# Attentions: ones beside the values, one set of matmuls for both, the result re-laid through memory

## The chip, the cores and the metric

The kernel runs on 1 core of one Trainium2 chip. The metric is the device time in microseconds (us) of one execution, compared between kernels on the same chip. The engines are called PE (TensorE), DVE (VectorE), ACT (ScalarE), POOL (GpSimd) and SP (SyncE, which only issues DMAs here).

## The reference

A model of four layers on x of 128 batches x 64 tokens x 128 features in f32. Each layer is a gated cross-attention of 16 heads of 8 features, then a gated feed-forward part. The attentions differ in details only (rotary embedding of keys and values in layer 0, biases in layers 1 and 3, a mask in layers 1 and 2); their core is the same:

```
def _L1_xattn_ref(q, k, v, mask, Wq, bq, Wk, bk, Wv, bv, Wo, bo):
    qh = _split_heads(q @ Wq.T + bq)
    kh = _split_heads(k @ Wk.T + bk)
    vh = _split_heads(v @ Wv.T + bv)
    scores = jnp.einsum('bhqd,bhkd->bhqk', qh, kh) * scale
    scores = jnp.where(mask == 0, jnp.float32(-1000000000.0), scores)
    probs = jax.nn.softmax(scores, axis=-1)
    attn = jnp.einsum('bhqk,bhkd->bhqd', probs, vh)
    concat = attn.transpose(0, 2, 1, 3).reshape(q.shape[0], q.shape[1], E)
    return concat @ Wo.T + bo
...
x = x + jnp.tanh(g_xattn[1]) * _L1_xattn_ref(_layernorm(x), ctx, ctx, mask, ...)
x = x + jnp.tanh(g_ffn[1]) * _L1_ffn_ref(_layernorm(x), ...)
```

The feed-forward parts are a routed mixture of experts with a shared expert (layer 0), a dense one (layer 1), a quantised linear one (layer 2) and a routed mixture (layer 3).

## The kernel before, in words

Tokens go in tiles of 128 (two batches), 64 tiles in all, and in chunks of 4 tiles (512 tokens), 16 in all. x stays in SBUF. An attention goes through the chunks in turns; a turn u has four steps s = 0..3, one for each tile, and each engine runs its own list of the turn, with semaphores between them. In layers 1 and 2 most turns stand in hardware loops of two turns (Fori); layers 0 and 3 are written out.

PE's turn (function attention, attention_quantised or attention_routed): at each s the scores of the tile two ahead (psS, L1199), at s = 1 the query projection q_proj of chunk u+1 (psQ, L1174), at s = 3 the transposes of the layer norm ln_t (psX, L1147), then p_turn (the exponentiated scores of the next tile turned into psT, 8 transposes, L1208) and weigh (the values weighed into psO, L1222, 16 matmuls of 64 columns). In layers 1 to 3 weigh also makes the row sums: 8 matmuls of 128 columns with a block of ones (ones2, L1228) into psY, already spread over the features. After it come v_proj of chunk u+1 at s = 0 (psQ; in layer 0 psQ and psY, L1167), k_proj of chunk u+2 at s = 2 (psQ, L1160) and out_proj of chunk u-1 at s = 3 (psX, L1258). A matmul in f32 whose weights or outputs use part of the array shows as two instructions.

ACT's turn: at each s p_high (psT to pT, L791) and exps (exp of the shifted scores, L785); q_out at s = 1, v_out at s = 0 (L762), k_out(u+2) at s = 2 (psQ to kT, L729), xt at s = 3 (L724), and at the end of the turn inverse(u): the reciprocal of the row sums as Exp(-Ln(.)) from psY into rden (L801, L803).

DVE's turn: at each s the shift (row maximum and subtraction, L1673, L1675), x_update(u-2) (L1695), layer norm statistics, and at the end of the turn normalise(u): aT = psO * rden (L1689). In layer 0 (SUMS) the row sums are made otherwise: DVE reduces the exponentials (sums, L1681, 128x1024, once a tile), ACT makes the reciprocals (L807, L811), PE turns them into psY (turn_rec, L1238) and ACT copies them out (L797). In the routed layers DVE also does the routing of finished chunks, and POOL scatters rows to memory (L609), behind the weighings. In layer 0 POOL rotates keys and values (rope_k, rope_v).

SP's turn (turn in attention on the sync engine): ctx_load(u+3) (L325), in layer 1 y_load, in layer 2 masks, then spread_k(u+2): it waits for k_out(u+2) (in layer 0 for rope_k) and issues 16 DMAs (L336), one for each head, from kT into the block-diagonal kexp, from which scores of chunk u+2 read. Two more chunks than there are (16 and 17) are spread at the end of each attention. Each stage ends with a barrier of all engines.

Of the kernel before, what the change touches and what calls it, by code (L numbers as in the profile page):

```python
# [7 lines left out]
F32 = mybir.dt.float32  # L8
# [13 lines left out]
LT = 4  # L22
# [18 lines left out]
N_INIT = 17  # L41
# [3 lines left out]
SUMS = (0,)  # L45
# [17 lines left out]
def program(nc, a, out):  # L63

    xg = nc.dram_tensor("xg", (XROWS, XW), F32, kind="Internal").ap()
    yg = nc.dram_tensor("yg", (YROWS, D), F32, kind="Internal").ap()

    with ExitStack() as ctx:
# [39 lines left out]
        ones2 = sb("ones2", [P, 2, 32])  # L108
# [4 lines left out]
        den = sb("den", [P, LT, H])  # L113
        rec = sb("rec", [P, LT, H, DH])
# [90 lines left out]
        den_ok, rec_ok, rec_t = map(sem, ("den_ok", "rec_ok", "rec_t"))  # L205
# [59 lines left out]

        def sum_base(lay):

            return CHUNKS * sum(n in SUMS for n in range(lay))
# [12 lines left out]
        def _(sp):  # L281
# [27 lines left out]
            def attention(lay):  # L309
# [27 lines left out]

                def masks(i, u):
# [105 lines left out]
        def _(pool):  # L444
# [20 lines left out]
            fill(ones2[:, :, :], 0.0)  # L465
            e.wait_ge(init, 12)
            for par in range(2):
                for hi in range(2):
                    fill(ones2[64 * par:64 * par + 64, hi, 16 * hi + DH * par:16 * hi + DH * par + DH], 1.0)
            e.wait_ge(init, 16)  # L470
# [235 lines left out]
        def _(act):  # L706
# [42 lines left out]
            def v_out(lay, i, u):  # L749
# [10 lines left out]
                for par in range(2):  # L760
                    rows_ = slice(64 * par, 64 * par + 64)
                    ins = e.activation(v2[rows_, u % 2, :, :].rearrange("p t (x y) -> p (t x) y", y=32)[:, :, DH * par:DH * par + DH],  # L762
                                       v3(psQ[rows_, :], 64), ACT.Copy)
# [28 lines left out]

            def inverse(lay, i, u):
                if lay in SUMS:
                    e.wait_ge(rec_t, val(i, u, 1, sum_base(lay) + 1))
                    e.wait_ge(at_sb, val(i, u, 1, K0 + lay * CHUNKS))
                    e.activation(rden[:, :], psY[:, :], ACT.Copy).then_inc(rd_ok, 1)  # L797
                    return
# [6 lines left out]
            def reciprocals(lay, i, u):  # L805
                e.wait_ge(den_ok, val(i, u, LT, LT * (sum_base(lay) + 1)))
                e.activation(den[:, :, :], den[:, :, :], ACT.Ln).then_inc(ln_d, 1)  # L807
                e.wait_ge(ln_d, val(i, u, 1, lay * CHUNKS + 1))
                if i is not None or u > 0 or sum_base(lay) > 0:
                    e.wait_ge(rec_t, val(i, u, 1, sum_base(lay)))  # L810
                e.activation(rec[:, :, :, :].rearrange("p t h d -> p (t h) d"),  # L811
                             den[:, :, :].rearrange("p t (h b) -> p (t h) b", b=1).broadcast_to([P, LT * H, DH]),
                             ACT.Exp, scale=-1.0).then_inc(rec_ok, 1)
# [11 lines left out]
            def attention(lay):  # L825
# [12 lines left out]
                def turn(i, u):  # L838
                    for s in range(LT):
                        if s == 1:  # L840
                            q_out(lay, i, u + 1)
                        if s == 3 and (i is not None or u + 2 <= CHUNKS):
                            xt(ATT[lay], i, u + 2)
                        p_high(lay, i, *ahead(u, s, 1))
# [5 lines left out]
                    inverse(lay, i, u)  # L850
# [7 lines left out]
                turn(None, CHUNKS - 1)  # L858

            def attention_quantised(lay):  # L860
# [25 lines left out]
                def turn(i, u):  # L886
                    inside = u < CHUNKS
                    quantised = 3 <= u < CHUNKS + 3
                    for s in range(LT):
                        if s == 1 and inside:  # L890
                            q_out(lay, i, u + 1)
                        if s == 3 and u + 2 <= CHUNKS:
                            xt(ATT[lay], i, u + 2)
                        if inside:
# [1436 lines left out]
```

## Time and profile before

| what | us |
|---|---|
| time, median of 3 runs | 3023.58 (3023.51 to 3025.56) |
| span of the profiled execution, first to last instruction | 2951.3 |
| PE busy | 2427.0 (82% of the span) |
| DVE busy | 1636.3 (55%) |
| ACT busy | 1385.7 (47%) |
| POOL busy | 983.8 (33%) |

The profiled execution has its own time only as its span; what lies around the span (3023.58 - 2951.3 = 72.3 us) is start and end of the program. The attentions stand at about 60 to 490 us (layer 0), 930 to 1268 (layer 1), 1765 to 2122 (layer 2) and 2130 to 2517 (layer 3). Busy is the time in which an engine computes; the square brackets at the end of a timeline row tell how long the engine was idle before and who released it. PEclk is the granted TensorE clock as a share of 2.4 GHz.

### The profile page before, as it was taken

What the parts mean: (1) busy time and instruction counts of PE and PEld (TensorE: products, weight loads), DVE (VectorE), ACT (ScalarE), POOL (GpSimd) and SP (SyncE); (2) the same over time, 40 slices, a digit from 0 to 9 for tenths busy, and PEclk for the clock granted to TensorE, in tenths of its full rate; (3) what the DMA queues carried; (4) which work ended last, traced back from release to release, by engine and by line L of the source; (5) the groups of instructions that cost most, each with busy time, mean ns of one, the idle gap of its engine ahead of it and who ended that gap; (6) DMA issues with size and microseconds to landing.
All of it is one profiled execution on the core that took longest, in us unless ns stands there. A gap on an engine that the chain in (4) does not pass through costs nothing. (4 is left out here: it accounts for less than half of the span.)

```text
span 2951.3 us, 72710 instructions
## 1 busy us (share of the span) xinstructions
PE 2427.0 (82%) x27302; PEld 1747.2 (59%) x27302; DVE 1636.3 (55%) x4333; ACT 1385.7 (47%) x2082; POOL 983.8 (33%) x1065
## 2 busy tenths in 40 slices
PE   4788785699996899989999987999788887088882
PEld 2455553488884555567777764666455555077872
DVE  3789997444443677722222215888668888133332
ACT  2555553233332566645454544666456664044441
POOL 4446775534442222100000000111212555544444
PEclk8999986899997999989999998999789998599996
DMA  3111111256663222100000001111111111256667
GB/s 106 23 23 39 43 42 33 83 170 195 200 190 118 66 57 57 36 5 0 0 0 0 0 13 40 42 42 42 38 30 29 50 53 52 85 177 196 190 191 227
DMA packets 143811, 220.06 MB, mean 75 GB/s; under 512 B 27178, under 2 KB 94514, under 8 KB 143027
## 3 DMA queue, kind: packets, MB, share of 16 engines
q1 hardware_dynamic: 96930, 90.25, 12.1%
q10 hardware_dynamic: 29232, 90.37, 9.7%
q0 software_dynamic: 17408, 36.21, 3.5%
q8 instruction: 154, 2.52, 0.4%
q14 instruction: 87, 0.70, 0.1%
HBM read 157.48 MB, written 43.61 MB: 68 GB/s over the span
## 5 line engine op out<-in xcount | busy, mean ns | idle before, releaser
L679 POOL DMA_INDIRECT yg<-ysb,yidx x288 | 280.0, 972 | 415.7 <-DVE ysb L2133 184.3
L1673 DVE TENSOR_REDUCE mx<-psS 128x16 f32<-128x1024 f32 x264 | 322.0, 1220 | 153.9 <-PE psS L1199 152.7
L791 ACT ACTIVATE work<-psT 128x1024 f32<-128x1024 f32 x260 | 265.9, 1023 | 246.1 <-PE psT L1208 243.8
L785 ACT ACTIVATE work<-work 128x1024 f32<-128x1024 f32 x264 | 278.2, 1054 | 148.9 <-DVE work L1675 143.6
L1199 PE MATMUL psS<-kexp,qT 64*64 64x512 f32 x2112 | 293.9, 627 | 58.0 <-DMA kexp<-kT 46.7
L1675 DVE TENSOR_TENSOR work<-psS,mx 128x1024 f32<-128x1024 f32 x264 | 323.2, 1224 | 9.0
L478 POOL TENSOR_TENSOR ve<-mv,eps 128x4 f32<-128x4 f32 x85 | 17.2, 203 | 922.5 <-DVE mv L1649 922.0
L1208 PEld LDWEIGHTS psT<-ident,work 128*128 128x128 f32 x2080 | 242.5, 147 | 126.1 <-issue 66.3
L1208 PE MATMUL psT<-ident,work 128*128 128x128 f32 x2080 | 291.8, 286 | 2.9 <-ACT work L791 2.4
L1532 PEld LDWEIGHTS psY<-w_ffn,work 128*128 128x128 f32 x2016 | 247.6, 192 | 9.3 <-DVE work L2104 1.2
L1532 PE MATMUL psY<-w_ffn,work 128*128 128x128 f32 x2016 | 248.4, 275 | 1.6 <-DVE ysb L2127 1.0
L609 POOL DMA_INDIRECT xg<-gio,posi x192 | 191.6, 998 | 106.1 <-issue 49.4
L1222 PE MATMUL psO<-work,v 128*32 128x64 f32 x8192 | 172.0, 226 | 19.5 <-issue 19.4
L1222 PEld LDWEIGHTS psO<-work,v 128*32 128x32 f32 x8192 | 130.8, 112 | 65.5 <-issue 64.0
L1565 PEld LDWEIGHTS psO<-w_ffn,work 128*128 128x128 f32 x1024 | 131.3, 192 | 61.2 <-issue 49.7
L1565 PEld LDWEIGHTS psY<-w_ffn,work 128*128 128x128 f32 x1024 | 131.9, 192 | 53.5 <-issue 53.5
L1497 PE MATMUL psX<-ident,xin 128*128 128x128 f32 x288 | 56.2, 278 | 99.9 <-DMA xin<-xg 98.6
L1660 DVE TENSOR_SCALAR xn<-x_sb,mv,rstd 128x128 f32<-128x128 f32 (+1 forms) x340 | 103.9, 369 | 62.2 <-POOL rstd L480 56.7
L1059 ACT ACTIVATE xgT<-psX 128x256 f32<-128x256 f32 x72 | 27.7, 384 | 235.4 <-issue 84.0
L1565 PE MATMUL psO<-w_ffn,work 128*128 128x128 f32 x1024 | 133.2, 276 | 4.8 <-ACT work L1011 4.8
L1011 ACT ACTIVATE work<-psT,b 128x512 f32<-128x512 f32 x128 | 88.0, 687 | 103.5 <-PE psT L1555 103.3
L1011 ACT ACTIVATE work<-psS,b 128x512 f32<-128x512 f32 x128 | 87.0, 686 | 100.4 <-PE psS L1555 100.3
(265 smaller groups left out, 4658.6 us busy)
## 6 DMA issues: line engine op xcount, KB each, us to landing
w_ffn<-in_wmoe ACTq DMA_DIRECT2D x72, 578.0 KB, 3.9
w_ffn<-in_wmoe ACTq DMA_DIRECT2D x72, 576.0 KB, 3.8
ctxT<-in_ctxT SPq DMA_DIRECT2D x76, 256.0 KB, 2.7
xin<-xg SPq DMA_DIRECT2D x144, 132.0 KB, 2.7
kexp<-kT SPq DMA_DIRECT2D x1152, 16.0 KB
gio<-yg SPq DMA_DIRECT2D x16, 512.0 KB, 4.2
work<-yg SPq DMA_DIRECT2D x16, 512.0 KB, 6.4
yg<-ysb,yidx POOLq DMA_INDIRECT x288, 3.2
```

What stands on the lines that cost most here:

```text
L609: e.indirect_dma_start(out=xg, out_offset=bass.IndirectOffsetOnAxis(ap=posi[:, g, c, t:t + 1], axis=0), in_=ring[g % 4][:, t, :], in_offse ...
L679: e.indirect_dma_start(out=yg, out_offset=bass.IndirectOffsetOnAxis(ap=yidx[:, b, t:t + 1], axis=0), in_=ysb[:, b, t, :], in_offset=None, ...
L785: e.activation(sc[:, s % 2], sc[:, s % 2], ACT.Exp).then_inc(p_ok, 1)
L791: e.activation(pT[:, s % 2, :], psT[:, :], ACT.Copy).then_inc(pt_ok, 1)
L1011: e.activation(hbuf[:, n % 4, :], psU[n % 4], ACT.Gelu, bias=b1[:, hb:hb + 1]).then_inc(f["act_ok"], 1)
L1199: m = e.matmul(psS[64 * half:64 * half + 64, 512 * k:512 * k + 512], qT[64 * k:64 * k + 64, b, c:c + SEQ], kexp[64 * k:64 * k + 64, b, :, ...
L1208: m = e.transpose(psT[:, r * P:(r + 1) * P], sc[:, s % 2, 2 * r:2 * r + 2, :].rearrange("p a b -> p (a b)"), ident[:, :])
L1222: m = e.matmul(psO[32 * c:32 * c + 32, s * P + 64 * half:s * P + 64 * half + 64], v2[:, b, 2 * s + half, 64 * c + 16 * hi:64 * c + 16 * hi ...
L1532: mm = e.matmul(psY[:, t * D:(t + 1) * D], mh[:, b, k * SLOT + t * P:k * SLOT + (t + 1) * P], w[:, d0 + k * D:d0 + (k + 1) * D], start=(k ...
L1565: m = e.matmul(y[:, t * D:(t + 1) * D], hbuf[:, n % 4, t * P:(t + 1) * P], w_ffn[:, 2048 + hb * D:2048 + (hb + 1) * D], start=(hb == 0 and ...
L1673: e.tensor_reduce(mx[:, :], src, AX, ALU.max).then_inc(s_max, 1)
L1675: e.tensor_tensor(sc[:, s % 2], src, over_keys(mx[:, :]), ALU.subtract).then_inc(s_sub, 1)
```

## The change

The 32 columns of v2 that a value matmul loads for a pair of heads held 16 columns of values and 16 zeros shared with its neighbour. Now the second 16 hold ones (written once at the start, fill), so that one matmul gives weighed values (16 rows) and row sums (16 rows). Each of the 16 matmuls is start and stop by itself; psO holds two tiles at a time (hi x 256 columns + s % 2 x 128). The row-sum matmuls of layers 1 to 3 and layer 0's sums, reciprocals and turn_rec go, with ones2, den, rec.

The rows of psO are no longer in the order of the features, so after steps 1 and 3 of a turn ACT copies psO into raw (heads_out) and after step 3 stores the 512 KB of the chunk to a DRAM tensor rawd[u % 2] from its own DMA queue. SP loads them back in the order of the features (heads_in: two DMAs of 256 KB, sums first) into vsum. inverse and normalise of chunk u-1 read vsum and move from the end of turn u-1 to step 2 of turn u, in all four layers with Ln and Exp. v_proj of layers 1 to 3 writes psY. In layer 1 and 2 the loops of SP cover fewer turns. The host no longer permutes the rows of the output weights.

The core of the diff:

```diff
+    rawd = nc.dram_tensor("rawd", (2, 2, P, CW), F32, kind="Internal").ap()
...
+                def heads_in(i, u):
+                    b = u % 2
+                    e_ = 16 * (lay * (CHUNKS // 2) + u // 2 + 1)
+                    sp.wait_ge(raw_st[b], e_ if i is None else i * 16 + e_)
+                    src = rawd[b].rearrange("h (c v j) n -> (h c) v j n", c=4, v=2)
+                    for v in (1, 0):
+                        sp.dma_start(vsum[:, v, :], src[:, v, :, :]).then_inc(raw_ld, 16)
...
                 def turn(i, u):
+                    if i is not None or u > 0:
+                        heads_in(i, u - 1)
                     ctx_load(i, u + 3)
...
-                with sp.Fori(0, CHUNKS // 2 - (2 if lay == 1 else 0)) as i:
-                    turn(i, 0)
-                    turn(i, 1)
-                if lay == 1:
-                    for u in range(CHUNKS - 4, CHUNKS):
-                        turn(None, u)
+                turn(None, 0)
+                turn(None, 1)
+                with sp.Fori(0, (CHUNKS - 6) // 2) as i:
+                    turn(i, 2)
+                    turn(i, 3)
+                for u in range(CHUNKS - 4, CHUNKS):
+                    turn(None, u)
+                heads_in(None, CHUNKS - 1)
...
+            for b in range(2):
+                for par in range(2):
+                    fill(v2[64 * par:64 * par + 64, b, :, :].rearrange("p t (x y) -> p (t x) y", y=32)
+                         [:, :, 16 + DH * par:16 + DH * par + DH], 1.0)
...
+            def heads_out(lay, i, u, h):
+                e.wait_ge(pv_ps, val(i, u, LT, K0 + lay * TILES + 2 * h + 2))
+                if h == 0 and (i is not None or u > 0 or lay > 0):
+                    n = 16 * (lay * (CHUNKS // 2) + (u + 1) // 2)
+                    e.wait_ge(raw_st[(u + 1) % 2], n if i is None else i * 16 + n)
+                e.activation(raw[:, :, 2 * P * h:2 * P * h + 2 * P], psO[:, :].rearrange("p (a n) -> p a n", a=2), ACT.Copy)\
+                    .then_inc(raw_ok, 1)
+                if h == 1:
+                    e.wait_ge(raw_ok, val(i, u, 2, lay * 2 * CHUNKS + 2))
+                    e.wait_ge(at_sb, val(i, u, 1, K0 + lay * CHUNKS))
+                    e.dma_start(rawd[u % 2].rearrange("h p n -> p h n"), raw[:, :, :]).then_inc(raw_st[u % 2], 16)
...
             def inverse(lay, i, u):
-                e.wait_ge(pv_ps, val(i, u, LT, K0 + lay * TILES + LT))
+                e.wait_ge(raw_ld, val(i, u, 32, 32 * (lay * CHUNKS + 1)))
                 e.wait_ge(at_sb, val(i, u, 1, K0 + lay * CHUNKS))
-                e.activation(rden[:, :], psY[:, :], ACT.Ln).then_inc(ln_d, 1)
+                e.activation(rden[:, :], vsum[:, 1, :], ACT.Ln).then_inc(ln_d, 1)
...
+                        if s == 2 and (i is not None or u > 0):
+                            inverse(lay, i, u - 1)
                         p_high(lay, i, *ahead(u, s, 1))
                         exps(lay, i, *ahead(u, s, 2))
                         if s == 0:
                             v_out(lay, i, u + 1)
                         if s == 2:
                             k_out(lay, i, u + 2)
-                    inverse(lay, i, u)
+                        if s % 2 == 1:
+                            heads_out(lay, i, u, s // 2)
...
-                    e.wait_ge(at_sb, val(i, u, 1, lay * CHUNKS + K0))
+                if s % 2 == 0 and (i is not None or lay + u + s > 0):
+                    e.wait_ge(raw_ok, val(i, u, 2, lay * 2 * CHUNKS + s // 2))
                 e.wait_ge(pt_ok, val(i, u, LT, lay * NT + s + 1 + K0))
                 for half in range(2):
                     for hi in range(2):
                         for c in range(4):
                             at = (c + 4 * hi) * P + 64 * half
-                            m = e.matmul(psO[32 * c:32 * c + 32, s * P + 64 * half:s * P + 64 * half + 64],
-                                         v2[:, b, 2 * s + half, 64 * c + 16 * hi:64 * c + 16 * hi + 32],
-                                         pT[:, s % 2, at:at + 64], start=(hi == 0), stop=(hi == 1))
-                for hi in range(0 if lay in SUMS else 2):
-                    for c in range(4):
-                        at = (c + 4 * hi) * P
-                        m = e.matmul(psY[32 * c:32 * c + 32, s * P:(s + 1) * P], ones2[:, hi, :], pT[:, s % 2, at:at + P],
-                                     start=(hi == 0), stop=(hi == 1))
+                            to = hi * 2 * P + s % 2 * P + 64 * half
+                            m = e.matmul(psO[32 * c:32 * c + 32, to:to + 64],
+                                         v2[:, b, 2 * s + half, 64 * c + 32 * hi:64 * c + 32 * hi + 32],
+                                         pT[:, s % 2, at:at + 64], start=True, stop=True)
...
             def normalise(lay, i, u):
                 e.wait_ge(y_ps, val(i, u, 1, K0 + lay * CHUNKS))
+                e.wait_ge(raw_ld, val(i, u, 32, 32 * (lay * CHUNKS + 1)))
                 e.wait_ge(rd_ok, val(i, u, 1, lay * CHUNKS + 1))
-                e.tensor_tensor(aT[:, :], psO[:, :], rden[:, :], ALU.mult).then_inc(at_sb, 1)
+                e.tensor_tensor(aT[:, :], vsum[:, 0, :], rden[:, :], ALU.mult).then_inc(at_sb, 1)
...
+                        if s == 2 and (i is not None or u > 0):
+                            normalise(lay, i, u - 1)
```

## Rows read from the trace of the kernel before

**Rows 1.** Windows: length, busy PE, PEld, DVE, ACT, POOL, then PEclk, DMA, GB/s.

```profile
1055.00:1073.70 18.70, 17.89 (x325) 11.13 (x321) 13.83 (x23) 12.31 (x16) 3.71 (x4) 1.00 0.21 57
...
2335.90:2357.30 21.40, 19.14 (x331) 12.77 (x331) 18.72 (x53) 12.88 (x19) 12.36 (x14) 1.00 0.21 56
...
312.50:339.00 26.50, 21.95 (x290) 14.49 (x290) 24.64 (x52) 13.75 (x21) 19.32 (x20) 0.87 0.16 41
```

**Rows 2.** Timeline, PE, layer 1: start, us, line, operation, [idle before, releaser].

```profile
1062.88 0.62 PE L1228 MATMUL psY<-work,ones 128*32 128x128 f32 x16
...
1063.43 0.41 PE L1194 MATMUL psS<-negm,ident 64*64 64x512 bf16 x4
...
1079.13 1.13 PE L1174 MATMUL psQ<-xT,w_att 128*128 128x512 f32 x2 [0.81 <-ACT v L762]
```

**Rows 3.** Timeline, ACT, layer 1, the same turn.

```profile
1068.26 0.67 ACT L729 ACTIVATE kT<-psQ,vec 128x512 f32<-128x512 f32 x1
...
1070.49 1.03 ACT L791 ACTIVATE work<-psT 128x1024 f32<-128x1024 f32 x1 [0.28 <-PE psT L1208]
...
1071.59 1.06 ACT L785 ACTIVATE work<-work 128x1024 f32<-128x1024 f32 x1
...
1072.55 0.58 ACT L801 ACTIVATE rden<-psY 128x512 f32<-128x512 f32 x1
...
1073.16 0.63 ACT L803 ACTIVATE rden<-rden 128x512 f32<-128x512 f32 x1
```

**Rows 4.** Timeline, SP's queue, layer 1, the same turn.

```profile
1068.95 10.68 SPq L336 DMA_DIRECT2D kexp<-kT  x16
...
1080.31 0.35 SPq L325 DMA_DIRECT2D ctxT<-in_ctxT  x1
```

**Rows 5.** Timelines of PE, DVE and POOL, layer 0, two successive turns.

```profile
296.05 1.09 PE L1199 MATMUL psS<-kexp,qT 64*64 64x512 f32 x8 [2.26 <-DMA kexp<-kT]
...
297.63 1.21 DVE L1681 TENSOR_REDUCE den<-work 128x16 f32<-128x1024 f32 x1
...
317.73 1.27 POOL L499 TENSOR_TENSOR v<-v,cosv 128x512 f32<-128x512 f32 x1 [4.72 <-ACT kv_rot L729]
```

**Rows 6.** Timeline, SP's queue, spreads of keys, layers 0 to 3.

```profile
206.31 10.67 SPq L336 DMA_DIRECT2D kexp<-kT  x16
...
470.39 10.67 SPq L336 DMA_DIRECT2D kexp<-kT  x16
...
974.87 12.03 SPq L336 DMA_DIRECT2D kexp<-kT  x16
...
1255.78 10.65 SPq L336 DMA_DIRECT2D kexp<-kT  x16
...
1812.66 10.70 SPq L336 DMA_DIRECT2D kexp<-kT  x16
...
2099.55 10.68 SPq L336 DMA_DIRECT2D kexp<-kT  x16
...
2167.79 11.54 SPq L336 DMA_DIRECT2D kexp<-kT  x16
...
2477.26 10.68 SPq L336 DMA_DIRECT2D kexp<-kT  x16
```

**Rows 7.** DMA landings: two loads at 2123.5 and 2124.0; the page's medians.

```profile
DMA to landing us min/median/max: 2.9/3.2/3.5
...
ctxT<-in_ctxT SPq DMA_DIRECT2D x76, 256.0 KB, 2.7
...
gio<-yg SPq DMA_DIRECT2D x16, 512.0 KB, 4.2
```

**Rows 8.** Timelines of PE and DVE at the ends of layers 0, 1, 3.

```profile
476.56 2.07 PE L1258 MATMUL psX<-w_att,aT 128*128 128x128 f32 x8 [0.29 <-ACT lgt L935]
...
1267.81 0.87 DVE L1645 BATCH_NORM_STATS2 st<-x_sb 128x6 f32<-128x128 f32 x4 [2.77 <-SPq L242]
...
2487.76 2.07 PE L1258 MATMUL psX<-w_att,aT 128*128 128x128 f32 x8 [0.29 <-ACT lgt L935]
```

More of the change, by code:

```diff
@@ L463, in _ @@
                 fill(v2[:, b, :, :], 0.0)
[L465 to L470, printed above, removed]
+            e.wait_ge(init, 11)
+            for b in range(2):
+                for par in range(2):
+                    fill(v2[64 * par:64 * par + 64, b, :, :].rearrange("p t (x y) -> p (t x) y", y=32)
+                         [:, :, 16 + DH * par:16 + DH * par + DH], 1.0)
+            e.wait_ge(init, 15)
             e.drain().then_inc(init, 1)
@@ L762, in v_out @@
                     ins = e.activation(v2[rows_, u % 2, :, :].rearrange("p t (x y) -> p (t x) y", y=32)[:, :, DH * par:DH * par + DH],
-                                       v3(psQ[rows_, :], 64), ACT.Copy)
+                                       v3(psY[rows_, :], 64), ACT.Copy)
                 ins.then_inc(q_ev, 1)
@@ L858, in attention @@
                 turn(None, CHUNKS - 1)
+                inverse(lay, None, CHUNKS - 1)
             def attention_quantised(lay):
@@ L893, in turn @@
                             xt(ATT[lay], i, u + 2)
+                        if s == 2 and 0 < u <= CHUNKS:
+                            inverse(lay, i, u - 1)
                         if inside:
@@ L902, in turn @@
                             to16(i, u)
-                    if inside:
-                        inverse(lay, i, u)
+                        if s % 2 == 1 and inside:
+                            heads_out(lay, i, u, s // 2)
                     if quantised:
@@ L977, in attention_routed @@
                             xt(ATT[lay], None, u + 2)
-                        if s == 3 and inside and lay in SUMS:
-                            reciprocals(lay, None, u)
+                        if s == 2 and 0 < u <= CHUNKS:
+                            inverse(lay, None, u - 1)
                         if inside:
@@ L992, in attention_routed @@
                             k_out(lay, None, u + 2)
-                    if inside:
-                        inverse(lay, None, u)
+                        if s % 2 == 1 and inside:
+                            heads_out(lay, None, u, s // 2)
             def route_exp(i, u):
@@ L1334, in turn @@
                             scores(lay, i, *ahead(u, s, 2))
+                        if s == 1 and inside and u >= 4:
+                            e.wait_ge(FQ["y16"], val(i, u, 1, -3))
                         if s == 1 and inside:
@@ L1345, in turn @@
                             weigh(lay, i, u, s)
-                        if s == 0 and inside and u >= 4:
-                            e.wait_ge(FQ["y16"], val(i, u, 1, -3))
                         if s == 0 and inside:
@@ L2000, in attention_routed @@
                                 shifted(gn)
-                        if lay in SUMS and inside and LT * u + s + 1 < TILES:
-                            sums(lay, None, *ahead(u, s, 1))
-                    if inside:
-                        normalise(lay, None, u)
             def r4(k):
@@ L2253 @@
     order = heads4.transpose(2, 1, 0, 3).reshape(-1)
-    back = heads4.transpose(1, 0, 2, 3).reshape(-1)
     def stack(*ms):
@@ L2287 @@
                            "L0_ffn_ln_gamma", "L0_ffn_ln_beta")):
-        vec[:, k] = arr(v).reshape(D)[back] if v.endswith("bv") else arr(v).reshape(D)
+        vec[:, k] = arr(v).reshape(D)
     arrays["vec"] = vec
```

69 lines of the change are left out of this document (17 added, 52 removed).

## Prediction

> **What bounds the kernel now.** The views were read in this order: busy time by stage, a turn of the layer 1 attention on PE, ACT and SP, the landings of the loads, then a turn of layer 0, the pitch of each layer, and the ends of the layers. A turn is four tiles; a layer has 16. The 16 small DMAs of spread_k come once a turn, so their starts are the pitch: from the third group of a layer to the last are 15 turns. They give (470.39 - 206.31)/10 = 26.4 us in the last ten turns of layer 0, (1255.78 - 974.87)/15 = 18.73 in layer 1, (2099.55 - 1812.66)/15 = 19.13 in layer 2, and (2477.26 - 2167.79)/15 = 20.63 in layer 3 [rows 6]. In layer 1 PE is busy 17.9 of the 18.7 us of a turn [rows 1], and the one hole of note is 0.81 us before the query projection, where PE waits for ACT to take the values out of psQ [rows 2]. So layers 1 to 3 look bound by PE. Layer 0 is not: PE stands 2.26 us waiting for kexp [rows 5], and DVE is busy 24.6 of 26.5 us [rows 1].
>
> A second loop lies just under PE. k_out of a key chunk ends at 1068.26 + 0.67 = 1068.93 [rows 3], SP starts spreading it at 1068.95, and its 16 issues take 10.68 us [rows 4]; only then is SP free for its next DMA. The change puts work into this loop, and this decides the forecast.
>
> **The change part by part.** *PE.* The row-sum matmuls go in layers 1 to 3: from 1062.88 to 1063.43 is 0.55 us a tile [rows 2], 2.2 us a turn, 16 x 3 turns: 106 us of PE time. The value matmuls stay as many and as large, with the ones in columns that held zeros, so they cost nothing more. The values of layers 1 to 3 are now projected into psY, so the 0.81 us hole goes too. PE would need 18.73 - 2.2 - 0.8 = 15.7 us in layer 1, 16.1 in layer 2 and 17.6 in layer 3. In layer 0 four transposes a turn go; they wait for ACT, and PE waits for kexp later anyway: nothing.
>
> *The new loop.* SP now begins turn u with the two loads of heads_in(u-1), behind spread_k(u+1). ACT's inverse(u-1) waits for both, and stands in the queue ahead of p_high, exps and k_out(u+2) at s = 2. k_out(u+2) releases the next spread_k. This closes in exactly one turn, with no PE in it. Its steps in layer 1: release 0.02; the spread 10.90 (mean of 15 groups like [rows 4]); SP's gap to its next DMA, 1080.31 - 1079.63 = 0.68 where the loop branches [rows 4] and 0.28 elsewhere, 0.41 on average; both loads landed 3.6 after the first issue; landing to ACT 0.14; Ln and Exp 0.61 + 0.63 = 1.24; p_high to exps 1071.59 - 1070.49 = 1.10; exps to what follows 0.97; k_out 0.67 [rows 3]. The sum is 19.05 us. Layer 2 has spreads of 10.78 on average and a k_out of 0.58: 18.84. Layer 3 has no loop branch and spreads of 10.98, p_high to exps 0.92, and 0.3 more for the logits: 19.1, and 19.3 because DVE, busy 18.7 us of a turn there [rows 1], must fit under it.
>
> The 3.6 us are the unknown of this sum. Two loads of this shape, issued 0.47 us apart, landed 2.9 and 3.5 us after their own issues, so 4.0 after the first, with a third load just ahead of them; the median of this shape is 2.7, that of a single load of 512 KB 4.2 [rows 7]. If the two don't slow each other it is 0.47 + 2.7 = 3.2, as one load of their bytes 4.2. I take 3.6, the pair without the third load. Each 0.1 us is 4.5 us of the kernel (45 turns).
>
> The Trainium skill ("DMA: Bandwidth & Descriptors", the section on the anatomy of one DMA) gives a fixed 2 us a transfer plus bytes at 436 GB/s, nearly all of it the receipt of the write. By it, as an estimate, a load of 256 KB takes 2.6 us and the pair 3.1; the rows of this case are above it, and the sum goes by them.
>
> So per layer: layer 1 15 x (19.05 - 18.73) = +5; layer 2 15 x (18.84 - 19.13) = -4; layer 3 15 x (19.3 - 20.63) = -20. The 3 us a turn that PE gives up becomes a wait for kexp: the next late thing is SP.
>
> *The store.* Two copies of psO by ACT (like the 0.6 us evictions of [rows 3]) and a store of 512 KB per turn from ACT's queue. The copy of the second half ends some 3.3 us after k_out, the store lands some 4.2 us later (taken from the 512 KB load), and SP asks for it at k_out + 11.3: 3.8 us of cover. Without it the excess would add to the loop one for one. The weighing of tile 2 waits for the first copy, which has PE's kexp wait as cover. Cost nothing.
>
> *Layer 0.* On DVE four row-sum reductions of 1.21 us a turn go, one of them directly ahead of the shift [rows 5]; the new inverse puts back some of that on ACT: the scores after the landing start at 296.05, the reduction at 297.63, and with 1.13 for it and 2.45 for the shift exps start at 301.2, 5.3 us after the landing; the new way is 2.55 from the landing of kexp to that of the loads, 1.24 and 0.96, 4.75. In the first turns (pitch 24.8) the shortest way round stays 24 to 25: nothing. In the last ten, GpSimd with its scatters is in a loop over two turns: the value rotation starts at 317.73, released by ACT [rows 5], 21.8 us after the landing; three reductions of 1.13 (start to start) less on DVE make this 18.9; behind it come 19.3 us of GpSimd work and 12.0 of spreading, so 50.2 for two turns, 25.1 each: 10 x 1.3 = -13, in all -14 with the early ones. Ends: 0, and 10 x (26.4 - 24.1) = -23 if the loop of one turn decides.
>
> *Ends of the layers.* The last heads_in stands behind the last (useless) spread_k. From its start S the attention is ready for the output projection at S + 10.7 + 0.3 + 3.6 + 0.14 + 1.24 + 0.7 = S + 16.7 (0.4 later where ACT or SP has a little more). Layer 0: 487.0 instead of 476.56, +10.4. Layer 1: projection and update (2.04 + 0.75) end at 1275.4 where the barrier now falls at 1267.8, +7.6. Layer 3: 2494.0 instead of 2487.76, +6.2 [rows 6, 8]. Layer 2, of the same build, is taken at +7. Together +31. What follows in each is a serial chain, so nothing hides it.
>
> *Start.* Four strided memsets of 512 elements for the small ones of before: +1.4 us. The reordered weights and fewer row permutations are done by the host: nothing.
>
> **Sum.** +1.4 + 5 - 4 - 20 - 14 + 31 = -0.6. The span of the profiled run is 2951.3 us and the median of the runs 3023.58; the 72.3 us around the span are taken as unchanged. Forecast 3023 us: 106 us of PE work gone and no measurable difference. (A measurement of this kernel tells 0.2%, 6 us, from no change.)
>
> **The rivals.** *PE's time arrives.* If the new loop is not closed as I read it, the next bound is the landing of kexp: the spread, 1.35 to its landing, 0.1, and 5.5 from the scores through shift and exps to k_out, 17.7 us. Layers 1 and 2 would save 15 and 20, layer 3 33, layer 0 16, the ends cost 33: 2972. For it: PE is busy nine tenths. Against it: the order of the instructions in SP's and ACT's queues.
>
> *Fast landings.* The two loads don't slow each other: 3.2 for 3.6, so 45 x 0.4 = 18 us less: 3005. That is also near what the page's rule on one DMA would make of it (3.1).
>
> *The PE clock (slower).* In layer 0, where PE waits each turn for kexp, the granted clock of a turn was 0.87 [rows 1]: stretches at 1.2 GHz after waits; the turns of layers 1 and 3 hold 2.4 GHz (1.00). After the change PE has one wait of some 2.3 us per turn, right before the scores of s = 2. If the stretch behind it runs at 1.2 GHz, scores, transposes, weighing and k_proj take 7.9 for 3.95 us, k_out becomes ready 10.0 instead of 8.1 us behind the spread, and the turn grows by 1.9 us. In half of the 45 turns this is +43: 3066. It decides from four such turns up. The Trainium skill ("TensorE: Matmul & The Clock Gate", HAM oscillation) describes this: a wait for data in every tile that returns the engine to its low clock each time; layer 0 agrees with it in part (0.87, not 0.5).
>
> *A late store (slower).* If 512 KB to memory take 8 us or more beside the small DMAs, SP waits for raw_st, about 1 us a turn over 60 turns, less what was gained: 3055.
>
> **How the numbers follow.** The forecast as worked out has 0.50; fast landings 0.15; PE's time arriving 0.13; the clock 0.12; the late store or other delays in the queues 0.10. The forecast's own range, from the landing (3.4 to 4.0), layer 0 (0 to -23) and the ends, is 3004 to 3045. The range of all is 2975 to 3060, which leaves out the first rival for the most part and half of the clock's. Faster by over 0.2%: 0.12 + 0.15 + 0.13 = 0.40. Within: 0.20. Slower: 0.18 + 0.12 + 0.10 = 0.40.
>
> **What would show it.** A pitch of spread_k of 19.0, 18.8 and 19.3 us in layers 1 to 3, and PE waiting for kexp once a turn in all of them. SP issuing heads_in directly behind the 16th DMA of a spread, both loads landed 3.6 us later, Ln starting on that landing, and spread, loads, inverse, p_high, exps, k_out back to back. Layer 0 at about 25.1. Ends of the layers 6 to 10 us later, relative to their last spread. Wrong would be: a pitch near 17.7 (the loop is not there), ACT's inverse not waiting for a DMA, a clock under 0.95 in layers 1 to 3, or SP waiting at raw_st.

## The result and the profile after

| kernel | time, us | against the kernel before |
|---|---|---|
| before | 3023.55 (3021.88 to 3025.56) | 1 |
| after | 3149.78 (3141.64 to 3156.76) | 1.0412 (1.0395 to 1.0429) |

The change makes the kernel 126 us slower. The forecast was 3023 in a range of 2975 to 3060. Some lines of the page of the profile after (engine, busy us, share; the chain that ended last; line, engine, operation, count, busy, mean ns, idle before and its releaser; DMA landings; "..." stands for lines left out):

```profile
span 3155.0 us, 66826 instructions
...
PE 2442.4 (77%) x24166; PEld 1742.5 (55%) x24166; DVE 1553.0 (49%) x4269; ACT 1442.6 (46%) x2194; POOL 986.7 (31%) x1064
...
SPq 10%; DMA 9%; PE 8%; issue 4%; DVE 3%; ACT 2%; POOL 1%; POOLq 1%; ACTq 1%; another core or an unknown queue 1%; DVEq 0%
...
L817 ACT ACTIVATE rden<-vsum 128x512 f32<-128x512 f32 x64 | 40.3, 630 | 332.6 <-DMA vsum<-rawd 332.6
...
gio<-yg SPq DMA_DIRECT2D x16, 512.0 KB, 6.0
```

The chain is now led by SP's queue and by DMAs, and the inverse (L817) waits 5.2 us on average for its load, 64 times. The loads into gio in layer 1, which the change does not touch, land after 6.0 us instead of 4.2. PE has 3136 instructions less and yet is busy 15 us longer than the 2427 of before: it ran more of them at the lower clock (the same scores took 659 ns on average instead of 627, the same transposes 301 instead of 286). The windows that answer [rows 1] (a turn of layer 1, one of layer 3, one of layer 0; columns as there):

```profile
1117.70:1139.50 21.80, 17.82 (x257) 11.06 (x256) 13.89 (x24) 12.99 (x19) 3.88 (x4) 0.91 0.34 96
2560.00:2582.00 22.00, 17.80 (x268) 11.71 (x267) 19.82 (x54) 14.10 (x21) 12.86 (x15) 1.00 0.35 102
352.40:379.90 27.50, 23.00 (x299) 14.76 (x295) 19.79 (x54) 16.15 (x26) 19.30 (x20) 0.81 0.26 78
```

And the turn of layer 1 step by step, first SP's queue (answers [rows 4]), then ACT (answers [rows 3]):

```profile
1117.74 11.07 SPq L332 DMA_DIRECT2D kexp<-kT  x16
1129.23 1.27 SPq L340 DMA_DIRECT2D vsum<-rawd  x2
...
1139.49 11.01 SPq L332 DMA_DIRECT2D kexp<-kT  x16
```

```profile
1135.74 0.63 ACT L817 ACTIVATE rden<-vsum 128x512 f32<-128x512 f32 x1 [4.46 <-DMA vsum<-rawd]
1136.40 0.63 ACT L819 ACTIVATE rden<-rden 128x512 f32<-128x512 f32 x1
1136.94 1.01 ACT L799 ACTIVATE work<-psT 128x1024 f32<-128x1024 f32 x1
1137.84 1.05 ACT L793 ACTIVATE work<-work 128x1024 f32<-128x1024 f32 x1
1138.79 0.68 ACT L737 ACTIVATE kT<-psQ,vec 128x512 f32<-128x512 f32 x1
```

The loop of the forecast is there, and it closes: spread 11.07, gap 0.42, from the first load's issue to the inverse 6.51, from there to the next spread 3.75, together 21.75 us, the distance of the two spreads. The forecast's own numbers for the four steps are 10.92, 0.41, 3.74 and 3.98. Three of the four agree within 0.3 us; the load is the one that is wrong.

The landing has a second effect on PE, which the forecast did not have. ACT's exponentials stand behind the late inverse, and PE, which has already waited for kexp, waits for them too (30.0 us in 13 of the 15 turns of layer 1, beside 28.5 for kexp). Behind this wait it runs at 1.2 GHz; the same eight transposes took 1.09 us earlier in the turn:

```profile
1138.94 1.97 PE L1220 MATMUL psT<-ident,work 128*128 128x128 f32 x8 [2.55 <-ACT work L793]
```

**Where the 126 us are.** The kernel before takes 2958 us on one chip and 3022 to 3027 on three others, so times are compared only with the kernel before on the same chip, and turns only in stages that don't differ between the chips. The two kinds differ in the shared-expert stage (55.7 us in e1, 107.2 in e5) and in the turn of layer 3 (20.63 against 21.77). The profile of before has the short stage, the 20.63 and a span of 2951, as the quicker kind has them, and its times are those of the slower kind. So it very likely came from another chip than its times; that, and not start and end of the program, is then the 72 us "around the span". Mean turn over 15 turns (third to last spread of a layer), and the stretch from a layer's last spread to the end of its stage:

| | layer 0 | layer 1 | layer 2 | layer 3 |
|---|---|---|---|---|
| turn, before | 26.16 | 18.73 | 19.12 | 21.77 |
| turn, after (e5) | 27.01 | 21.55 | 21.26 | 21.86 |
| 15 turns, difference | +13 | +42 | +32 | +1 |
| same, forecast | -14 | +5 | -4 | -20 |
| end, difference | +12 | +12 | +9 | +9 |
| same, forecast | +10 | +8 | +7 | +6 |

(Before: e1 for layers 0 to 2, e11, the kernel before with an addition in layer 0 alone, for layer 3. The last end is taken together with the expert stage behind it, to which 26 us of the work passes. The other profile of after has 27.11, 21.54, 21.48 and 22.22 us a turn, so a difference over 15 turns is sure to some 5 us.) The sum is +130; the other stages give back 7 (the feed-forward 486.6 instead of 490.1 us, routed and shared experts of layer 0 together 4 less). That makes 123, where the two pairs of times have 126 and 119.

### The profile page after: what moved, and what is told of

Read it like the earlier page. It is cut to its first block and busy times, and to the rows that moved or that the text cites. A ratio compares the mean times of both kernels' runs of the same rounds, so it can differ in the third digit from the quotient of the medians.

```text
span 3155.0 us, 66826 instructions
## 1 busy us (share of the span) xinstructions
PE 2442.4 (77%) x24166; PEld 1742.5 (55%) x24166; DVE 1553.0 (49%) x4269; ACT 1442.6 (46%) x2194; POOL 986.7 (31%) x1064
## 5 line engine op out<-in xcount | busy, mean ns | idle before, releaser
L1211 PE MATMUL psS<-kexp,qT 64*64 64x512 f32 x2112 | 311.0, 659 | 105.8 <-DMA kexp<-kT 78.8
L1220 PEld LDWEIGHTS psT<-ident,work 128*128 128x128 f32 x2080 | 260.5, 156 | 211.2 <-ACT work L793 108.0
L1220 PE MATMUL psT<-ident,work 128*128 128x128 f32 x2080 | 315.9, 301 | 74.8 <-ACT work L793 62.9
L1236 PE MATMUL psO<-work,v 128*32 128x64 f32 x8192 | 190.5, 237 | 3.8 <-issue 3.8
L817 ACT ACTIVATE rden<-vsum 128x512 f32<-128x512 f32 x64 | 40.3, 630 | 332.6 <-DMA vsum<-rawd 332.6
L1236 PEld LDWEIGHTS psO<-work,v 128*32 128x32 f32 x8192 | 143.4, 119 | 54.5 <-issue 53.6
L1211 PEld LDWEIGHTS psS<-kexp,qT 64*64 64x64 f32 x2112 | 74.5, 142 | 157.3 <-issue 145.4
```

Of the source, the lines that this page charges most:

```text
L1211: m = e.matmul(psS[64 * half:64 * half + 64, 512 * k:512 * k + 512], qT[64 * k:64 * k + 64, b, c:c + SEQ], kexp[64 * k:64 * k + 64, b, :, ...
L1220: m = e.transpose(psT[:, r * P:(r + 1) * P], sc[:, s % 2, 2 * r:2 * r + 2, :].rearrange("p a b -> p (a b)"), ident[:, :])
L1236: m = e.matmul(psO[32 * c:32 * c + 32, to:to + 64], v2[:, b, 2 * s + half, 64 * c + 32 * hi:64 * c + 32 * hi + 32], pT[:, s % 2, at:at + 6 ...
```

## The experiments

**e1_before and e5_after: both kernels once more.**

> The kernel before once more, to compare stage by stage from the same day. In its first profile the span was 2951.3 us and the median time 3023.6, 72 us apart; in the profile of the changed kernel the two are 1.8 us apart, and its shared-expert stage is 109 us long against 55. Theory A (the first profiled execution simply missed a stall that the timed ones have): this profile has a span near 3021, and the 70 us lie in a few places, the shared-expert stage among them. Theory B (the change costs the shared-expert stage 54 us): the span is again 2950 and the stage 55 us.

Measured: 2958.7 us (before beside it 2957.9), profiled span 2963.9, shared-expert stage 55.7 us. Span and stage are as theory B has them, yet not for its reason, as e5 and e11 show: a chip of the other kind has the long stage with the kernel before too.

> The changed kernel once more, beside the kernel before. In the second profile of the kernel before, the time and the span agree (2958.7 and 2963.9 us) and its shared-expert stage is 56 us long, as in e2, e3 and e4; only the first trace of the changed kernel has 110 there. Theory A (the change doesn't touch that stage): it is 56 us here, turns of 21.5, 21.5 and 22.2 us in layers 1 to 3, and the time is e2_load16's 3024.7 + 45 x 1.8 = 3105 (3090 to 3120). Theory B (the change stalls it): 110 us again and a time above 3150.

Measured: 3145.8 us, 1.0396 (1.0376 to 1.0417) of the 3027.0 beside it, 107 us in the shared-expert stage. Neither theory holds as written. The stage is as long in e11, which is the kernel before in all but layer 0, on a chip of this kind; so it belongs to the chip and not to the change, and e5 is not 3105 because it ran on a chip of the slower kind, e2 on the other. The windows of the stage, e5 and then e1 (columns as above):

```profile
537.20:644.40 107.20, 59.23 (x256) 38.68 (x256) 38.44 (x96) 23.05 (x33) 46.81 (x48) 0.74 0.09 31
```

```profile
509.50:565.20 55.70, 51.95 (x256) 34.73 (x256) 38.90 (x96) 23.16 (x33) 42.02 (x43) 0.93 0.16 52
```

The same work takes twice the time, with hardly a busy us more on DVE or ACT. What stretches it was not found.

**e2_load16: the loads with 16 outermost.**

```diff
-src = rawd[b].rearrange("h (c v j) n -> (h c) v j n", c=4, v=2)
+src = rawd[b].rearrange("h (c v j) n -> v j (h c) n", c=4, v=2)
```

(and the rows of the output projection's weights in the matching order)

> The changed kernel with one thing different: the two loads of vsum walk memory with a dimension of 16 outermost (j, then h and c) instead of one of 8 (h and c, then j). Same bytes, same 2 KB rows, same place in SP's queue; the partitions of vsum come in another order and the rows of the output projection's weights are permuted to it. Theory A (a load whose slowest dimension is 8 runs on 8 of the 16 DMA engines, as its 9 instead of 16 semaphore updates say): the pair lands 3.4 to 4.0 us after the first issue instead of 5.3 to 6.4, the turns of layers 1 to 3 take 18.9 to 19.4 us instead of 21.5 to 22.2, and the time is 3149.8 - 45 x 2.4 - 8 at the ends, about 3030 (3015 to 3045). Theory B (the loads are slow because they read what was just written, or stand behind the 16 small DMAs of the spread): the landing stays near 6 us and the time near 3150.

Measured: 1.0224 (1.0201 to 1.0246) of before, 3024.7 us beside 2957.9. SP's queue, then ACT:

```profile
1066.73 11.23 SPq L332 DMA_DIRECT2D kexp<-kT  x16
1078.38 1.23 SPq L340 DMA_DIRECT2D vsum<-rawd  x2
```

```profile
1083.06 0.63 ACT L817 ACTIVATE rden<-vsum 128x512 f32<-128x512 f32 x1 [4.35 <-DMA vsum<-rawd]
```

From issue to inverse 4.68 us instead of 6.51. Mean landing of the pair over 15 turns, by the semaphore updates in the trace: 6.4, 6.5 and 6.3 us in layers 1 to 3 of the profile after, 4.6 in all three here. The turns take 19.83, 19.72 and 20.29 us. Theory A holds for the cause: with the order of the dimensions changed and nothing else, the landing is 1.8 us shorter. It is too hopeful for the size: 4.6 us lies above its 3.4 to 4.0, and the turns of layers 1 and 2 lie above its 19.4. That the time of 3024.7 us lies in its range is luck, since the range was worked out from times of the slower kind of chip; against the kernel before, 4.1% more became 2.2% more.

The trace shows the two kinds of load apart: one of the kernel after makes 9 updates of its semaphore, one here 16. The Trainium skill ("DMA: Bandwidth & Descriptors", the section on why a DMA increments its semaphore by 16) says why: a DMA from SP or ACT runs on the largest number of engines up to 16 that divides the slowest dimension on both sides, and the rest of the 16 increments is written at once. With 8 outermost that is 8 engines and 8 + 1 updates. The forecast drew on this page for the time of one DMA, and left out this rule of it, the one that speaks against the change. The trace agrees with it in the number of updates, and the landing in its direction (6.4 against 4.6 us); which engines carried the bytes the trace does not tell.

**e12_rows_walk and e10_one_load: the last microsecond.** e12 reads the rows as they lie in memory and so leaves out the re-laying and the reciprocal; e10 makes one load of the pair.

> e2_load16 with loads that read the rows of rawd in the order in which they lie there (128 rows, one behind the other) instead of j first with steps of 64 KB between the heads' rows. Same bytes, same rows of 2 KB, written as recently, 16 engines. The rows then arrive at other partitions than they should, so the re-laying is left out of what is computed, and the logarithm is a copy (of the same length) with the exponent scaled by 0.0001, so that all numbers stay finite. In e2 the pair lands 4.6 us after the first issue and in e10 the single load 4.8 us, where the forecast had 3.6 and 4.2. Theory A (the walk in 64 KB steps costs it): the pair lands in 3.6 to 4.0 us, turns of 18.9 to 19.3 us in layer 1. Theory B (what counts is that the memory was written a few us before, or the traffic beside the loads): 4.4 to 4.7 us, turns of 19.7 to 19.9 us.

Measured: 1.0048 (1.0026 to 1.0071), 3037.9 us beside 3023.4. SP's queue, then ACT:

```profile
1114.50 0.81 SPq L340 DMA_DIRECT2D vsum<-rawd  x2
...
1122.02 10.83 SPq L332 DMA_DIRECT2D kexp<-kT  x16
```

```profile
1117.92 0.63 ACT L817 ACTIVATE rden<-vsum 128x512 f32<-128x512 f32 x1 [2.01 <-DMA vsum<-rawd]
```

The pair lands in 3.4 us on average in layers 1 and 2 (0.4 of it is won in the issue, 0.81 for both instead of 1.23), and the turns take 18.85 and 18.48 us. Theory A holds in layers 1 and 2 (the landing is even a little shorter than its 3.6 to 4.0), theory B falls: what was written a few us before landed in 3.4 us for the pair, and the two loads from older memory in [rows 7], with a third just ahead of them, in 4.0. The steps of 64 KB of e2 cost 1.2 us. In layer 3 the turn of 20.82 us is that of e10 (20.88) on this kind of chip, so there the quicker landing buys nothing more.

> e2_load16 with the pair of loads of 256 KB made one load of 512 KB, 16 outermost as before. In e2 the pair landed 4.6 us after the first issue, 1.0 above the 3.6 of the forecast. Theory A (the excess is the bytes and the write receipt of two transfers on the same engines; the second issue, 0.64 us, is not hidden): one load lands about 4.2 us after its issue, as the other load of 512 KB did, and frees SP 0.6 us earlier, turns of 19.4 instead of 19.8 us. Theory B (the excess comes from reading what was written a few us before, or from the 64 KB strides of the walk): 4.6 us or more, turns unchanged.

Measured: 1.0183 (1.0166 to 1.0201); the load lands 4.8 us after its issue on average in layers 1 and 2 (4.3 to 5.3); turns of 19.93 and 19.64 us in layers 1 and 2. Theory A falls: one DMA instead of two gains nothing.

**e4_no_trip: everything but the trip.**

```diff
-e.dma_start(rawd[u % 2]..., raw[:, :, :]).then_inc(raw_st[u % 2], 16)
-for v in (1, 0):
-    sp.dma_start(vsum[:, v, :], src[:, v, :, :]).then_inc(raw_ld, 16)
```

> The changed kernel without the trip through memory: neither store nor loads; the inverse and the normalisation read a vsum that is set to one at the start (this leaves out the re-laying, so the output is not the attention's; the arithmetic on every engine stays). Theory A (the trip is all that costs, the matmuls' saving is real): turns of layers 1 to 3 of 17.5 to 18 us, time 2950 to 2985. Theory B (TensorE's saving is eaten by its clock, which falls at the kexp wait): turns near 19 and a granted clock under 0.95 in these layers, time above 3000.

Measured: 0.9906 (0.9882 to 0.993), 2928.3 us beside 2957.9. The turns take 18.14, 18.07 and 19.87 us: theory A in layers 1 and 2 nearly, not in layer 3, whose turn has another bound. A turn of layer 1:

```profile
1044.00:1062.00 18.00, 15.73 (x255) 9.56 (x253) 14.06 (x23) 13.27 (x17) 3.75 (x4) 1.00 0.24 58
```

Thirteen of the 15 turns of layer 1 take 17.8 to 18.0 us, and PE waits for kexp in each of them: this is kexp's loop, which the forecast put at 17.7. PE is busy 15.7 us in the turn shown and 16.2 on average in the layer (17.6 before), and the clock holds at 1.00 (0.99 in the layer). So the matmuls' saving is real, but smaller than the forecast had it: from the start of the weighing to the next work of PE it is 1.02 us before (1062.41 to 1063.43) and 0.59 here (1049.01 to 1049.60), that is 0.43 us a tile and not 0.55, some 83 us of PE's work in layers 1 to 3 and not 106. Of these 43 come through (10, 20 and 13 of span), because the next bound lies just under the old one.

**e3, e6 and e8: taking the loads out of the loop.** In short, not in the code's own lines (the condition on the turn differs from layer to layer):

```diff
+if s == 1 and 0 < u: heads_in(lay, i, u - 1)      # e3: ACT issues them
-if s == 2 ...: inverse / normalise                # e6: SP issues them as before,
+if s == 3 ...: inverse / normalise                #     both a tile later
+heads_in(lay, None, CHUNKS - 1)                   # e8: e6, last pair by ACT
```

> As e2_load16, and the two loads are issued by ACT at the head of s = 1 instead of by SP behind the 16 DMAs of spread_k, so that the loads no longer stand in the loop k_out, spread_k, loads, inverse, k_out. Theory A (that loop sets the turn): the next bound is the landing of kexp with the scores and exponents behind it, 17.7 us a turn by the forecast's first rival, so the time falls to about 2970 (2950 to 2995), 50 below e2_load16. Theory B (what sets the turn is something else, TensorE at a lower clock or ACT's own queue, which gets two more issues of some 0.45 us): no more than 15 us below e2_load16.

Measured: 1.0304 (1.0277 to 1.0331), turns of 20.66, 20.78 and 21.88 us: 25 us slower than e2, where 50 less were expected. Queues of SP and ACT, and PE:

```profile
1079.88 10.72 SPq L332 DMA_DIRECT2D kexp<-kT  x16
```

```profile
1089.26 1.18 ACTq L809 DMA_DIRECT2D vsum<-rawd  x2
```

```profile
1094.59 0.64 PE L1210 MATMUL psS<-negm,ident 64*64 64x512 bf16 x4 [3.98 <-DMA kexp<-kT]
1094.98 1.95 PE L1215 MATMUL psS<-kexp,qT 64*64 64x512 f32 x8
```

The spread is issued by 1090.60, but PE gets kexp at 1094.6. In layer 1 the last kexp landed some 1.35 us behind its issue on average in every other kernel, and 3.0 us in this one: half a MB of loads was issued just ahead of its last DMAs. PE then waits 4 us and starts at 1.2 GHz (scores 1.95 instead of 1.05 us; the granted clock of the layer is 0.91 against 0.95 in e2). The loop through the loads is broken, and the cost is paid in that of kexp. How this cost divides between the later landing and the clock was not tried.

> e2_load16 with the inverse on ACT and the normalisation on DVE moved from s = 2 to s = 3, behind k_out; the loads stay behind spread_k on SP, where they can't hold up kexp's landing (in e3 the last kexp landed 3.7 us after its issue instead of 1.35, beside the loads). Theory A (the loop k_out, spread_k, loads, inverse, k_out sets the turn in e2): turns of 17.9 to 18.2 us in layers 1 and 2 and 19.9 in layer 3, as in e4_no_trip, and 2928 + 40 for the ends of the layers = 2970 (2960 to 2985). Theory B (the turn is held by the loads' bytes or TensorE's clock): turns of 19 us or more, time above 3005.

Measured: 1.0049 (1.0029 to 1.0068), 3042.7 us beside 3027.0, turns of 18.36, 19.02 and 20.93 us. Theory A nearly holds in layer 1 (17.9 to 18.2 was expected), goes half way in layer 2 (19.72 in e2), and fails in layer 3, where e7 and e10 have 20.91 and 20.88 on this kind of chip without it. The absolute times of the expectation are of the other kind of chip.

> e6_late_inverse with the last pair of loads of each layer issued by ACT as soon as the store has landed, instead of by SP behind the last spread, which nobody reads. Theory A (the ends cost what the order in SP's queue costs): the stretch from the last spread to the end of the stage falls from 47, 21, 32 and 48 us by 8, 3, 4 and 3 us as in e3, so 15 to 20 us less than e6_late_inverse, about 2952, level with the kernel before (2958) or just under it. Theory B (the useless spread's DMAs slow these loads down instead): no less than e6_late_inverse.

Measured: 0.9973 (0.9959 to 0.9986), 3017.3 us. That is 25 us less than e6, beyond theory A's 15 to 20. The ends fell from 46, 21, 32 and 72 to 37, 17, 27 and 64 us. What the late inverse costs is seen on PE: in layer 1 it waits 1.16 us for aT in 14 of the 15 turns, and 1.1 instead of e4's 1.6 us for kexp. This is a likely reason why the turn is 18.43 us and not the 18.14 of e4; it was not tried by itself.

```profile
1142.52 1.16 PE L1270 MATMUL psX<-w_att,aT 128*128 128x128 f32 x8 [1.16 <-DVE aT L1691]
```

**e7, e9 and e11: TensorE's clock.**

```diff
+for n in range((3, 2, 2, 2)[lay]):
+    e.matmul(psT[:, 0:512], ident[:, :], w_att[:, 0:4, :], start=True, stop=True)
 scores(lay, i, *ahead(u, s, 2))      # at s = 2, where PE waits for kexp
```

> e2_load16 with idle matmuls (ident times 512 columns of w_att, into psT, which is overwritten next) on TensorE ahead of the scores that wait for kexp: 3 a turn in layer 0, 2 in layers 1 to 3, some 3.3 and 2.2 us, inside its wait. They change no result. Theory A (the wait costs TensorE its clock, and in layer 0 this is why a turn takes 27.2 us instead of 26.5): the granted clock of layer 0 rises from 0.82 to 0.9 or more and its turn falls by 1 us or more; in layer 1 all turns take 19.4 instead of 19.3 to 20.5; together 25 to 50 us less than e2_load16. Theory B (the clock is beside the point, the loops don't go through TensorE): within 8 us of e2_load16, or slower.

Measured: 1.0113 (1.0091 to 1.0134), 3059.9 us on the slower kind of chip, where e10 (e2 in all but the number of loads) took 3078.5. Layer 0, 15 turns, of e2 and then of e7:

```profile
82.90:487.10 404.20, 328.83 (x4301) 210.37 (x4300) 270.38 (x655) 232.83 (x343) 238.53 (x234) 0.82 0.26 72
```

```profile
88.40:469.50 381.10, 330.06 (x4390) 201.45 (x4378) 290.48 (x657) 231.03 (x343) 240.28 (x233) 0.98 0.27 77
```

The clock goes from 0.82 to 0.98 and the turn from 26.94 to 25.41 us. In layers 1 and 2 the clock goes from 0.95 to 1.00 and the turn stays, at 19.84 and 19.82; in layer 3 it stays too (0.95 and 20.88 in e10, 1.00 and 20.91 here). Theory A holds for layer 0 and falls for layer 1: where the loop passes through SP and the loads, PE's clock has slack. One wait of layer 0 in the profile after, and the scores behind it at 1.2 GHz:

```profile
365.57 1.98 PE L1211 MATMUL psS<-kexp,qT 64*64 64x512 f32 x8 [3.87 <-DMA kexp<-kT]
```

> The kernel before with 3 of the same idle matmuls a turn in layer 0, ahead of the scores that wait for kexp; layers 1 to 3 hold 1.00 there and get none. Theory A (the stretch at 1.2 GHz is in its layer 0 too, clock 0.88, but DVE and GpSimd set the turn): the clock goes to 0.95 or more and the turn falls by no more than 0.5 us, 0 to 8 us in all. Theory B (the clock sets the turn here as in the changed kernel): 15 us or more less than the kernel before, and the gain of e9 over the kernel before is then mostly this.

Measured: 0.9973 (0.996 to 0.9986), 3014.1 us beside 3022.2. Layer 0 of e1, then of e11:

```profile
81.30:473.70 392.40, 319.76 (x4365) 208.85 (x4363) 347.25 (x716) 218.55 (x328) 238.87 (x233) 0.88 0.14 34
```

```profile
84.70:468.30 383.60, 329.24 (x4457) 204.42 (x4455) 356.87 (x716) 217.89 (x329) 239.01 (x233) 0.99 0.14 35
```

That is 9 us less in layer 0, 8 in all: at the edge of theory A, far from B's 15. With the clock held, layer 0 takes 25.57 us a turn before the change and 25.41 after it. The gain here is all in the first five turns (25.38 to 23.83); the last ten take 26.55 us in e1 and 26.44 with the clock held.

> e8_late_ends with the idle matmuls of e7 in the two layers whose granted clock was under 0.95 (3 a turn in layer 0, 2 in layer 3). Theory A (e7 took layer 0 from 26.9 to 25.4 us a turn by the clock alone; layer 3 of e8 has 0.94 and 21.2 us a turn): layer 0 falls from 26.5 to 25.3 us a turn, layer 3 by 0.5 us or more, so 20 to 30 us less than e8_late_ends: 0.989 to 0.993 of the kernel before. Theory B (in e8 other loops stand just below): within 8 us of e8.

Measured: 0.9949 (0.993 to 0.9968), 3005.7 us beside 3022.2; layer 0 takes 25.64 instead of 26.51, layer 3 20.86 instead of 21.23 us a turn. The turns together are 20 us shorter, at the lower end of theory A; the time is only 7 to 12 us less than e8's (by the ratios and by the times, on different chips), near theory B's 8. It is the fastest kernel here with the whole computation, 0.2% under e11, with intervals that touch: the change's idea, mended in four places, is worth hardly more than three idle matmuls a turn in layer 0 of the old kernel.

## Why the prediction was wrong

The turns of layers 1 and 2 came out 73 us over the forecast, layer 0 27, layer 3 21 and the ends 11; the other stages gave back 7. Together that is 125 of the 126 us.

- *The new loop.* Right in place, order and members: [rows 3, 4, 6] gave it, and e12, with a landing of 3.4 us in place of 3.6, has turns of 18.85 and 18.48 us where the forecast had 19.05 and 18.84. PE waiting for kexp once a turn, no wait of SP for the store, Ln starting on the landing: as foretold. PE's second wait, for the exponentials, was not; with it one of the forecast's signs of being wrong came true, a clock under 0.95 (0.93, 0.95 and 0.93 over the turns of layers 1 to 3 of the profile after, 0.91 in the turn of layer 1 shown).
- *The 3.6 us from the first issue to the landing of both loads.* This is the step that failed. The term measured 6.4 (15 turns each of layers 1 to 3), 2.8 more. It was taken from [rows 7], loads of the same bytes and the same partitions but with 128 rows outermost in memory. Shape meant bytes there, and should have meant the order of the dimensions. In layers 1 and 2 the 2.8 us are 84 us, at the four ends 11 more. (The turns of the two layers are 73 us over and not 84, since the other steps were a little shorter.) e2 shows 1.8 of them go with twice the engines although its walk is the worse one (steps of 64 KB against 16 rows in order of memory); e12, with both mended, shows 3.0. How the 3.0 divide between engine count and walk was not measured by one alone, since 8 outermost with e2's walk was not tried.
- *The rule of one DMA.* With 3.1 us for the pair it stood near the rival of fast landings (3.2, rated at 0.15); e12 comes to 3.4, the kernel itself never near it. 16 updates a load are not enough for it: e2 has them and takes 4.6.
- *Layer 0.* Forecast 25.1 us a turn for its last ten (26.4 before) and no change in the first five (24.8); measured 27.3 and 26.4 in e5. e2 has 27.3 and e4 27.2 in the last ten, so the trip has hardly a part in them. With the clock held they take 25.5 us (e7) against 26.4 for the kernel before (e11): there the steps taken from DVE come through, 0.9 of the 1.3 us, and without that the slower PE takes them back. PE waits longer for kexp than before (4.7 us a turn in e2, 2.9 in e1), and the slow stretch behind the wait, which cost 0.1 us a turn before the change, costs 1.8 after it. In the first five turns the changed kernel is slower even with the clock held (25.2 against 23.8); why is open. Layer 0 is thus the second step that failed, 27 us over the forecast: the forecast let PE's clock there cost nothing.
- *The PE clock.* This rival, rated at 0.12, was placed in layers 1 to 3. In layers 1 and 2 it costs nothing in e2 (e7 shows it; for the kernel after itself, where the longer landing leaves PE more slack, it is argued). It decided in layer 0, where the row of 0.87 in [rows 1] had already shown it. The Trainium skill ("TensorE: Matmul & The Clock Gate", HAM oscillation) describes just this, a wait for data in every round after which the engine restarts slow; layer 0 of e2 (0.82) and e7 (0.98) agree.
- *Layer 3.* Forecast 20 us less. Against a before of the same kind of chip it is 1 more with the slow load and 14 less in e12 (20.82 against 21.77). Only a part of the miss is the landing: the 19.3 us a turn are not reached by any run, and e4, without loads and on the quicker kind of chip, still takes 19.87. The bound that the forecast guessed from DVE's busy time lies higher; what it is was not found.
- *Ends.* +31 forecast, +42 measured; 11 is what the landing adds at four ends.
- *PE's saving.* 106 us forecast, some 83 by the steps of e4: the interval of 0.55 us between two starts was taken for what goes, but 0.12 of it stays as the end of the weighing. It did no harm, since PE does not set the turn after the change.
- *Start.* +1.4 forecast; SP issues the load of layer 0's weights at 15.42 instead of 13.60 us.
- *Around the span.* The 72.3 us were very likely a difference of chips. It did no harm to the difference of the kernels outside layer 3, but it is no property of the program. That layer 3 was forecast from 20.63 us, while the times came from a chip with 21.77, comes of the same mistake.
- *The rivals.* "PE's time arrives" had the right bound (17.7, in e4 17.9), which shows once the loads are gone. "A late store" did not occur. The range ended at 3060 since the sum let the landing be no more than 0.4 us over its value, and the row of 4.2 us for a load of 512 KB was taken for a bound from above, which it was not. The same page of before has other loads of 512 KB at 6.4 us, and the forecast does not name them:

```profile
work<-yg SPq DMA_DIRECT2D x16, 512.0 KB, 6.4
```

## What to carry to other kernels

Before a DMA is priced by a row of the same size, write down the slowest dimension of both its sides and the walk in memory: inside a loop that closes once a turn, 8 outermost made 4% more time of the change, 16 outermost with steps of 64 KB 2%, and rows in order of memory 0.5%. Moving bulk loads to another queue did not keep them out of the way of the small DMAs (their last landing went from 1.35 to 3.0 us): put them behind the transfer that somebody waits for, not ahead of its tail. And a turn whose granted clock is under 1 before a change is a place where less work on other engines may buy nothing until PE's wait is filled: in the last ten turns of layer 0 the low clock was free before the change and cost 1.8 us a turn after it.

## What the runs showed of the hardware

- The same pair of loads of 256 KB landed after 6.4 us with 8 outermost (9 semaphore updates a load), after 4.6 with 16 outermost and steps of 64 KB (16 updates), and after 3.4 in order of memory (16 updates); issuing both took 1.27, 1.23 and 0.81 us.
- Reading back memory that was written a few us before showed no price of its own (3.4 us for the pair in e12, 4.0 for the pair of [rows 7]).
- A wait of PE of 4.0 us was followed by scores at 1.2 GHz (e3, 1.95 us) and one of 2.55 us by transposes at 1.2 GHz (after, 1.97), one of 1.7 us in e4 by scores at full speed (1.05). In layer 0 of before a wait of 2.26 us was followed by scores of 1.09 us, one of 2.39 us a turn later by scores of 1.80. The rows of e4:

```profile
1056.36 0.41 PE L1199 MATMUL psS<-negm,ident 64*64 64x512 bf16 x4 [1.73 <-DMA kexp<-kT]
1056.57 1.05 PE L1204 MATMUL psS<-kexp,qT 64*64 64x512 f32 x8
```

- Chips differed by 64 to 69 us for one program: +53 in the shared-expert stage, +17 in layer 3's turns, -9 from that stage to the end of layer 0's routed experts. GpSimd's scatters are in the first two, but also in layer 0's attention, where e2 and e10 agree across the chips (26.94 and 26.98 us a turn). Why was not tried.
